# Shorter router product, an earlier scale chain, the last hid turned on TensorE, and shared down products one entry later

## What is computed

```python
x = x + xattn(layernorm(x), ctx_512, Wq, Wkv_expand, Wout)     # x: 8 x 512 x 512, ctx: 8 x 64 x 128
x = x + ffn(layernorm(x), ...)
# xattn: 16 heads of 32, 64 keys, causal mask, softmax, output projection
# ffn, T = 4096 tokens, H = 512, E = 8 experts, I = 256, K = 2:
logits = x @ router_w.T
scores, top_idx = top_k(logits, 2)
comb[t, top_idx] = scores
g, u = einsum('td,edi->eti', x, wg), einsum('td,edi->eti', x, wu)
y = einsum('eti,eid->etd', silu(g) * u, wd)
moe_out = einsum('etd,te->td', y, comb)
se = (silu(x @ sg_w + sg_b) * (x @ su_w + su_b)) @ sd_w + sd_b
out = moe_out + se
```

## Time and profile before

| | |
|---|---|
| median of 3 runs | 814.28 us (812.19 to 814.79) |
| profiled execution: time, span | 817.98 us, 815.9 us |
| mean granted TensorE clock | 0.985 of full speed |
| busy: PE, DVE, ACT, POOL | 768.2 (94%), 579.2 (71%), 458.1 (56%), 427.5 (52%) us |
| attention stage | up to about 342 us |
| shared entries (some steps among them) | about 342 to 492 us |
| routed entries | about 492 us to the end |

### The profile page before, as it was taken

The page is one execution under the profiler, slowest core; times in us unless marked ns, Lnnn a source line. Parts: engine busy times, 40 slices in busy tenths (PEclk is TensorE's granted clock), DMA queues, the critical chain, the costliest instruction groups (busy, mean ns, idle before and its releaser), DMA issues.

```text
span 815.9 us, 22099 instructions
## 1 busy us (share of the span) xinstructions
PE 768.2 (94%) x7372; PEld 526.0 (64%) x7372; DVE 579.2 (71%) x1190; ACT 458.1 (56%) x844; POOL 427.5 (52%) x530
## 2 busy tenths in 40 slices
PE   3888999999999999899999999999999999999994
PEld 1566878888888888767778875545554555555551
DVE  4889899999999998835788775555555555565552
ACT  1857888999898889765546533333333333333330
POOL 1425777777767777434110012556555556556643
PEclk9999999999999999999999999999999999999997
DMA  8224688777777686858746554879899899989982
GB/s 284 91 68 142 193 215 221 203 223 211 226 206 199 201 232 170 226 146 241 247 156 204 184 206 111 139 144 154 146 154 147 150 146 152 155 133 162 151 137 31
DMA packets 138861, 140.85 MB, mean 173 GB/s; under 512 B 88416, under 2 KB 89440, under 8 KB 138400
## 3 DMA queue, kind: packets, MB, share of 16 engines
q1 hardware_dynamic: 122880, 104.14, 47.7%
q0 software_dynamic: 15904, 35.70, 25.3%
HBM read 71.61 MB, written 52.31 MB: 152 GB/s over the span
## 4 chain that ended last, share of the span: by engine, by line
PE 79%; DVE 10%; DMA 4%; issue 3%; ACT 2%; POOL 1%; SPq 1%; another core or an unknown queue 0%; DVEq 0%; POOLq 0%; ACTq 0%
PE psum L1388 45%; PE psum L1446 16%; PE psum L1379 9%; PE psum L1492 4%; DMA hidT<-xn2p 3%; PE psum L1525 2%; DMA exp_all<-routerT 1%; DVE stats L1025 1%; DVE mags L910 1%; DVE kv_store L942 1%; DVE hid L1343 1%; DVE head_max L1101 1%; DVE xy L1119 1%; DVE hidT L942 0%; PE psum L1495 0%
## 5 line engine op out<-in xcount | busy, mean ns | idle before, releaser
L719 POOL DMA_INDIRECT out<-w_q,tabs x71 | 112.5, 1584 | 110.5 <-DVE w_q L1368 77.5
L709 POOL DMA_INDIRECT x_in<-normed_tokens,tabs x71 | 70.6, 995 | 93.9 <-DVE tabs L1253 44.5
L893 ACT ACTIVATE silu_g<-psum,tabs 128x256 f32<-128x256 f32 x71 | 33.6, 473 | 145.5 <-PE psum L1388 133.2
L1353 DVE SCALAR_TENSOR_TENSOR hid<-psum,tabs,silu_g 128x256 f32<-128x256 f32 x71 | 34.4, 484 | 110.9 <-ACT silu_g L893 109.3
L1388 PE MATMUL psum<-exp_all,hidT 128*128 x426 | 104.3, 382 | 4.1 <-DMA hidT<-xn2p 4.0
L1388 PE MATMUL psum<-exp_all,probsT 128*128 x420 | 96.4, 379 | 0.0
L1446 PE MATMUL psum<-xn1T,w_q 128*128 128x128 f16 x1536 | 91.0, 219 | 1.3 <-DVE w_q L942 1.3
L1388 PE MATMUL psum<-w_o,attnT 128*128 128x512 f16 x384 | 89.3, 382 | 0.0
L1446 PEld LDWEIGHTS psum<-xn1T,w_q 128*128 128x128 f16 x1536 | 86.3, 98 | 2.6 <-issue 2.4
L577 POOL TENSOR_TENSOR exp_all<-piece,exp_all 128x512 f32 (+1 forms) x48 | 56.1, 1169 | 53.4 <-ACT piece L739 53.4
L1388 PEld LDWEIGHTS psum<-exp_all,hidT 128*128 128x128 f16 x426 | 41.7, 98 | 55.7 <-issue 7.4
(11 more groups left out here) (204 smaller groups left out, 1656.3 us busy)
## 6 DMA issues: line engine op xcount, KB each, us to landing
x_in<-x SPq DMA_DIRECT2D x64, 256.0 KB, 3.2
exp_all<-experts SPq DMA_DIRECT2D x24, 512.0 KB, 4.5
out<-xy SPq DMA_DIRECT2D x32, 256.0 KB, 2.5
normed_tokens<-xn SPq DMA_DIRECT2D x32, 256.0 KB, 4.5
normed_turned<-xn2T SPq DMA_DIRECT2D x32, 256.0 KB, 2.7
w_q<-out SPq DMA_DIRECT2D x32, 256.0 KB, 3.3
out<-w_q SPq DMA_DIRECT2D x32, 256.0 KB, 2.5
probsT<-normed_turned SPq DMA_DIRECT2D x16, 256.0 KB, 3.0
```

The lines of the kernel that those rows point to most:

```text
L709: pool.indirect_dma_start(x_in[:, t % 4, :], None, xn_dram, bass.IndirectOffsetOnAxis(gather_at[:, t:t + 1], 0)).then_inc(gathered[t % 4], 16)
L719: pool.indirect_dma_start(out, bass.IndirectOffsetOnAxis(add_at[:, t:t + 1], 0), y[:, t % Y_RING, :], None, bounds_check=TOKENS - 1, oob_i ...
L893: act.activation(silu_g[:, :], psum[:, GU_BANK[m % 2], 0:I], ACT.Silu, scale=gate_scale_at[:, tm:tm + 1]).then_inc(silu_ready, 1)
L1353: dve.scalar_tensor_tensor(hid[:, :], psum[:, GU_BANK[m % 2], I:2 * I], up_scale_at[:, tm:tm + 1], silu_g[:, :], ALU.mult, ALU.mult).then_ ...
```

## The change

1. **Router.** The 12 matmuls of 8 columns become 8: with the high part of xn2T as weights one matmul of 16 columns makes both products (with w_r high and w_r low), with the low part one of 8 columns. ScalarE copies 16 columns to `logit_terms` (two buffers), and GpSimd adds the two halves into `logits`, a new operation in each step. SP's store of the logits, which waits for it, moves behind the DMA transpose of xn2p.
2. **Scale chain.** `expert_scales` 0 and 1 move from j = 1 into j = 0, ahead of and behind the residual; `from_dram` moves to the head of SP's step. The other five stay.
3. **Last hid.** The last routed entry's hid is turned by TensorE (two transposes into PSUM bank 4), copied by ScalarE and subtracted by VectorE instead of going through hid_parts and the DMA transpose.
4. **Down products.** Shared ones run in entry k+3, as the routed ones do, and their hidT uses all four buffers. SP's stores and base loads of y move one entry back with them.

```diff
 def down_at(n):
-    k = n - 2 if n - 2 < T else n - 3
-    return k if 0 <= k < ENTRIES and not (k == T - 1 and n == T + 2) else None
+    return n - 3 if elive(n - 3) else None
...
 # SP
+                if j == 0 and found(b - 2) is not None:
+                    from_dram(b - 2)
                 if live(tile + 1) and not (isinstance(b, int) and (b, j) == (0, 0)):
                     load_x(tile + 1, j + 1)
...
-                if 0 <= n - 3 < T:
-                    store_shared(n - 3)
-                if n < T:
-                    load_base(n)
+                if 0 <= n - 4 < T:
+                    store_shared(n - 4)
+                if 0 <= n - 1 < T:
+                    load_base(n - 1)
...
-                if t < SLOTS:
+                if t < SLOTS - 1:
                     turn_hid(t)
 # GpSimd, in step, before inv_std(1, t4)
+                if live(t6):
+                    pool.wait_ge(terms_ready, t6 + 1)
+                    plain(pool)
+                    pool.tensor_tensor(logits[:, bass.ds(t6, 1), :].rearrange("p o e -> p (o e)"), logit_terms[:, j % 2, 0:E],
+                                       logit_terms[:, j % 2, E:2 * E], ALU.add).then_inc(logits_ready, 1)
 # ScalarE
+                    wait(act, logits_ready, t6 - 1)
+                    copy(logit_terms[:, j % 2, :], psum[:, 6, 0:2 * E], sc[:, S_R:S_R + 1], terms_ready)
...
+                if tk == SLOTS - 1:
+                    act.wait_ge(last_mm, 1)
+                    act.wait_ge(down_mm, T + tk - 3)
+                    copy(flat(hidT[:, tk % 4, 0, :, :]), bank(LAST_BANK)[:, 0:I], 1.0, last_hi)
 # VectorE
+                if begun is not None:
+                    expert_scales(begun, 0)
                 if live(t4):
...
                     stage_stats(1, x1, t4)
+                if begun is not None:
+                    expert_scales(begun, 1)
...
+                if tk == SLOTS - 1:
+                    dve.wait_ge(last_hi, 1)
+                    dve.tensor_tensor(flat(hidT[:, tk % 4, 1, :, :]), bank(LAST_BANK)[:, 0:I], flat(hidT[:, tk % 4, 0, :, :]),
+                                      ALU.subtract).then_inc(last_ready, 1)
 # TensorE
-                    product(psum[:, 6, 0:E], chunks(xn2T), columns(w_r, E), C, router_mm)
+                    both_parts = w_r[:, :, :].rearrange("p v (c e) -> p c v e", c=C)
+                    for c in range(C):
+                        for a in ((0, 1), (1, 0))[c == C - 1]:
...
+                if n == ENTRIES + 1:
+                    pe.wait_ge(hid_ready, ENTRIES)
+                    pe.wait_ge(xgT_ready, SLOTS)
+                    transposes(bank(LAST_BANK), hid, CI, last_mm)
```

More of the change, by code:

```diff
@@ L511, in _ @@
                     entry(2 * (tile - T) - 3)
-            for n in range(2 * LAG - 4, T + 3):
+            for n in range(2 * LAG - 4, T + 4):
                 entry(n)
@@ L620, in step @@
                 tile = TPB * b + j
-                t2, t3, t4, t5 = [tile - n for n in range(2, 6)]
+                t2, t3, t4, t5, t6 = [tile - n for n in range(2, 7)]
                 e, pieces = pieces_at(b, j)
@@ L882, in entry @@
                         act.wait_ge(hid_ready, m + 1)
-                        wait(act, down_mm, m - 1)
-                        copy(flat(hidT[:, m % 2, 0, :, :]), hid[:, :], sc[:, S_HID:S_HID + 1], hidT_hi)
+                        wait(act, down_mm, m - 3)
+                        copy(flat(hidT[:, m % 4, 0, :, :]), hid[:, :], sc[:, S_HID:S_HID + 1], hidT_hi)
                         if HOT_AT <= n < HOT_AT + QUADS:
@@ L1073, in step @@
                     low(flat(qT[:, 1, :, :]), bank(5), Q_DOWN, flat(qT[:, 0, :, :]), qT_ready)
-                if scaled is not None:
-                    expert_scales(scaled, 0)
                 if live(t4):
@@ L1079, in step @@
                                       ALU.subtract).then_inc(attnT_ready, 1)
-                if scaled is not None:
-                    expert_scales(scaled, 1)
                 if live(t3):
@@ L1347, in entry @@
                         dve.wait_ge(hidT_hi, m + 1)
-                        low(flat(hidT[:, m % 2, 1, :, :]), hid[:, :], col(sc, S_HID), flat(hidT[:, m % 2, 0, :, :]), hidT_ready)
+                        low(flat(hidT[:, m % 4, 1, :, :]), hid[:, :], col(sc, S_HID), flat(hidT[:, m % 4, 0, :, :]), hidT_ready)
                     else:
@@ L1505, in step @@
                     pe.wait_ge(xn2_turned, 16 * (t6 + 1))
-                    wait(pe, logits_ready, t6)
+                    wait(pe, terms_ready, t6)
                     if isinstance(t6, int) and t6 == 0:
                         pe.wait_ge(wsh_split, 1)
-                    product(psum[:, 6, 0:E], chunks(xn2T), columns(w_r, E), C, router_mm)
+                    both_parts = w_r[:, :, :].rearrange("p v (c e) -> p c v e", c=C)
+                    for c in range(C):
+                        for a in ((0, 1), (1, 0))[c == C - 1]:
+                            if a == 0:
+                                last = pe.matmul(psum[:, 6, 0:2 * E].rearrange("p (v e) -> p v e", v=2), xn2T[:, 0, c, :],
+                                                 both_parts[:, c, :, :], start=(c == 0), stop=(c == C - 1))
+                            else:
+                                last = pe.matmul(psum[:, 6, 0:E], xn2T[:, 1, c, :], w_r[:, 0, c * E:(c + 1) * E],
+                                                 start=False, stop=False)
+                    last.then_inc(router_mm, 1)
                 if live(t4):
@@ L1587, in entry @@
                     tk = ranked(k)
-                    if tk is None:
+                    if tk == SLOTS - 1:
+                        pe.wait_ge(last_ready, 1)
+                    elif tk is None:
                         pe.wait_ge(hidT_ready, k + 1)
@@ L1595, in entry @@
                     if tk is None:
-                        product(bank(DOWN_BANK[k % 2]), chunks(hidT[:, k % 2]), columns(w_sh, H, GU), CI, down_mm)
+                        product(bank(DOWN_BANK[k % 2]), chunks(hidT[:, k % 4]), columns(w_sh, H, GU), CI, down_mm)
                     else:
```

21 lines of the change are left out of this document (11 added, 10 removed).

## The result

| | before | changed |
|---|---|---|
| median of 4 runs | 813.43 us (812.19 to 814.79) | 802.60 us (802.09 to 803.22) |
| profiled execution: time, span | 817.98, 815.9 us | 803.22, 801.5 us |
| busy: PE, DVE, ACT, POOL | 768.2, 579.2, 458.1, 427.5 us | 759.7, 581.1, 457.4, 433.1 us |
| mean granted TensorE clock | 0.985 | 0.992 |

A forecast was written before the change was run, and what follows sets the result against it. TensorE was taken to set the attention stage's pace, VectorE only 8% behind. Terms -1.5 - 0.1 - 0.8 - 1.6 - 0.5 - 4.8 + 0.8 - 2.2 gave -10.7 us, 803.5 against 814.28; 8-in-10 range 800.0 to 808.5.

The forecast's parts named there:

- Router and scale chain in the loop: Attention loop: -0.39 + 0.31 - 0.17 = -0.25 us per batch element, six giving -1.5; the lone router step ahead -0.1.
- So three of four steps gain: 0.39 us per batch element: Attention loop: shorter router saves TensorE 0.13 us per step, except j = 3, where it turns into waiting.
- This edit alone loses: Attention loop: moving the scale chain into j = 0 costs 0.31 us of TensorE waiting and returns 0.17 per batch element.
- Last steps: Batch element 8, end of attention: VectorE's chain loses 0.65 us, one router ahead is shorter, attn comes 0.78 us earlier: -0.8.
- Clock: First shared gate product: TensorE's idle time falls to about 1.55 us, so the clock stays up: -1.6 us, bounds 0 and -1.63.
- Routers of tiles 34 to 37: Routers of these four tiles: the shorter router gives -0.5 us.
- hidT: Shared entries, 340 to 500 us: later down products remove all 5.0 us of waits, 0.2 left for new lateness: -4.8 us.
- First turn: Start of routed stage: first transpose of routed hid stands behind the last store of shared y, so its product waits: +0.8 us.
- Tail: Kernel end: last hid turned on TensorE lets the last additions start earlier: -2.2 us, between -1.5 and -3.0.
- the slow SP queue: Rival, attention steps: SP waits for logits behind GpSimd's addition, delaying later loads, stores and turns; slower, 818 us; chance 0.05.
- VectorE lengthened the j = 0 step: Rival: VectorE takes TensorE's place in every attention step, 7 us come back, 811 to 814 us; chance 0.05.
- the waits for hidT took no other name: Rival, shared entries: hid or y comes late instead, half of the 5.0 us comes back, 806.0 us; chance 0.08.

The follow-up runs named there:

- e6_late: The changed kernel with the reduction over mag_rows behind attn in j = 0 and the small operation behind it in j = 1; ratio 0.9882 to the kernel before.
- e1_router: The kernel before with the router part alone; ratio 1.0004.
- e10_filled: The kernel before with six unread matmuls of 512 columns in TensorE's 2.38 us wait for attn ahead of the first shared gate product; ratio 0.9982.
- e4_down: The kernel before with the shared down products one entry later and hidT in four buffers alone; ratio 0.9943.
- e7_turnfirst: The changed kernel with the first turn of routed hid issued ahead of the last store of shared y; ratio 0.9873 to the kernel before.
- e3_lasthid: The kernel before with the last hid turned on TensorE alone; ratio 0.9976.
- e9_router_einv: The kernel before with the router part alone and einv moved from ahead of the reciprocal to behind attn; ratio 0.9989.
- e8_both: The changed kernel with the late reduction and the first routed hid turned ahead of the last store of shared y; ratio 0.9848 to the kernel before.

## Why the forecast was right, and where it was not

The sum was right, in part since its errors cancelled: the terms came out at -1.6, -0.4, -1.3, -0.3, -5.6, +1.0 and -2.4, in all -10.6 us. One by one:

- **Router and scale chain in the loop (-1.5, and -0.1 ahead of it).** The six batch elements took 229.60 us in the profile before and 227.99 in the one after, -1.6. They are not alike: the first is 0.60 us shorter, the second 0.44, the usual later one 0.2 (38.19 to 37.97), and one of 38.32 us gained nothing. The lone step ahead of them gave nothing (9.87 and 9.89 us). The two steps by which I came to the term were wrong apart, and their errors cancelled. "So three of four steps gain: 0.39 us per batch element" fails: the router alone lost 0.3, since einv fell in with the key copy. And "This edit alone loses" fails: the chain's move gained 0.1 alone and 0.48 beside the short router. I had followed the 0.65 us of the two operations that move and taken the durations of the five that stay for fixed. Without einv held or the reduction in the way (e6_late) the short router gives 0.3 us (38.19 less the 0.17 us wait, against 37.70), and j = 3 takes part, as j = 0 doesn't: its step stayed at 9.37 us in e1_router and e6_late. The early reduction costs 0.27 us there for the forecast 0.31.
- **Last steps (-0.8).** Mis-sized: the two steps took 9.45 + 9.08 us and take 9.62 + 8.50, -0.4 us. "One shorter router is ahead of its qT" gave nothing: with the router alone that step took 9.12 us and the wait grew to 2.54. The step with j = 0 pays 0.17 us here too, as in the loop, which I had left out. And of the 0.65 us that left VectorE's chain 0.24 came back: epow, an operation that stayed, took 0.40 us (at 335.89) where it had taken 0.16. So the idle time was 2.09 us and not the forecast 1.55.
- **Clock (-1.6).** The size is shown by e10_filled (1.62 us). That it came was luck in part: "An idle time of 1.55 us lies on the harmless side of both" rests on a time that was not reached, and 2.04 us were not harmless in two other kernels. With the clock up, the product was ready before its load and waited 0.30 us, so about 1.3 came.
- **Routers of tiles 34 to 37 (-0.5).** From the last transposes of attn to the last router 23.56 us (e4_down) became 23.36, and one more router lies ahead of them: -0.3, though each router got 0.19 us shorter and not 0.13.
- **hidT (-4.8).** It was more, and nothing went back. From the last transposes of attn to the first gather it is 127.61 us in e1_router, which has the same router, and 122.05 in the changed kernel: -5.6. I had added up the idle times, and the start-to-start distances are longer.
- **First turn (+0.8).** 1.0 us, and e7_turnfirst shows that the store ahead of it was the cause. I had taken 2.4 us from the turn to its product, where the row that I named has 2.55; with it the sum gives 1.0.
- **Tail (-2.2).** The working's own times, 808.43 and 806.1, give -2.3. It is -2.4 between the two profiles, -1.5 to -2.7 against the six that have the old tail, and -2.0 in e3_lasthid's times. Both additions come at 0.30 us and 1.55 us, as estimated.

Alone the four parts give +0.3 - 2.3 - 2.0 - 4.6 = -8.6 us, the whole -10.8. Each of these differences has an uncertainty of some 2 us, so the missing 2.2 are not shown by the times. The profiles show 1.2 of them in the six batch elements of the loop: 229.60 us before, 230.47 with the router alone, 228.28 with the chain's move alone and 227.99 with both. What carries this are the loop's lengths, which repeat to 0.1 us from one batch element to the next but for single ones (37.76 and 38.32 in the changed kernel, 37.99 in e1_router).

Of the rivals, the slow SP queue did not show (no wait for x_in in the loop), VectorE lengthened the j = 0 step by 0.18 us and no other, and the waits for hidT took no other name in the changed kernel.

## What to carry to other kernels

Test the parts of a change also apart: here the sum was right while both halves of one term had the wrong sign, and a part that shortens one engine's work by 0.19 us moved two others into each other for 0.42. Before work is moved to where an engine "has room", list the short operations on VectorE's path that run beside GpSimd's long ones, and keep them apart by order, not by hundredths of a microsecond. Where TensorE must stand still for about 2 us ahead of a long product, a few matmuls that nobody reads can keep its clock; they did in the three kernels here that had them, and cost nothing, since they ended 0.80 to 1.24 us before attn came.

## What the runs showed of the hardware

**A VectorE operation on two numbers is held until GpSimd's copy beside it ends, or not at all.** Over 12 of the 14 kernels (in the other two it stands behind attn), einv (from SBUF to SBUF, two numbers per partition) began beside a key copy in 64 steps. In 21 it began at most 0.03 us behind the copy's start in the trace: 0.15 us each, and the copy took 0.62 to 0.66 us. In 9 it began 0.04 to 0.07 us behind: 0.57 to 0.60 us. In 22 it began 0.30 to 0.47 us behind and took 0.17 to 0.33 us. In these 31 it ended 0.02 to 0.04 us behind the copy. In the other 12 it began with the copy nearly done and took its 0.15 us. Reciprocals, which read PSUM, were not held: they took 0.24 or 0.25 us in every kernel, also the one in e9_router_einv that began 0.06 us behind the copy. In the changed kernel the pair meets late in the copy and costs 0.07:

```profile
263.11 0.61 POOL L608 COPY kv_store<-kv_store 32x512 f16 x1 [0.24 <-POOL kv_store L608]
...
263.52 0.22 DVE L1067 TENSOR_SCALAR einv<-epow  x1
```

The Trainium skill ("SBUF — State Buffer", Who interferes with whom) has this as an exclusive lock on a port pair that VectorE and GpSimd share, taken for the whole instruction by the one that starts first, and names tensor_scalar among the operations that can take it. The 31 held cases agree. In 18 of the 21 that were not held einv began 0.01 to 0.03 us behind the copy by the trace, so who came first can't be read from it there.

**Einv was not the only one.** In the changed kernel epow, also on two numbers and in the same j = 1 step, falls in with GpSimd's low part of xn2 takes 0.61 to 0.68 us in each batch element of the loop, where it took 0.15 or 0.16 before, and ends with GpSimd's operation:

```profile
259.91 1.16 POOL L642 TENSOR_TENSOR xn2p<-xn,xn2p 128x512 f16<-128x512 f32 x1
...
260.41 0.68 DVE L1064 TENSOR_SCALAR epow<-emax 128x2 int32 x1
```

It costs TensorE at most some 0.1 us of a batch element: the j = 1 and j = 2 steps are 9.32 and 9.75 us here, and 9.27 and 9.70 in e6_late, where epow takes 0.16. In e6_late it is the first operation on emax that is held, for 0.89 us. The two operations of the chain on one number per partition took 0.14 to 0.22 us in all 224 cases, 79 of them well inside an operation of GpSimd. And a GpSimd operation on one column (`rstd<-rstd,minus_half`) held none of the two-number ones that began beside it (19 cases).

**The length of a wait alone doesn't decide the clock.** Behind 2.38, 2.39, 2.39, 2.52, 2.53 and 2.54 us of waiting for attn the granted clock fell to 0.50 (1.2 GHz), and behind 0.80, 1.09, 1.24, 1.71 to 1.82 and 1.90 us it stayed at 1.00 (2.4 GHz). Between them the order breaks: behind 2.04 us (e6_late, e8_both) it fell, behind 2.09 and 2.11 (the changed kernel, e7_turnfirst) it stayed. Of the two steps ahead of the wait, the first took 9.43 us in the former two and 9.62 in the latter, the second 8.63 and 8.50. In the fallen cases the lower level came between 0.3 us before and 1.4 us behind the restart. What tells them apart stays open; the three kernels that filled the wait all kept the clock.
